# New per-half tiles, new engine lists and a moved addition in a four-layer attention and expert kernel on one core

## The reference, cut to what matters

```python
x0 = x; y = ln_c(x)                            # no gain, no bias
for i in range(4):
    x_s = attention(layernorm(y, gs, bs), w_qkv_s, w_out_s, b_out_s)      # over 64 positions
    x_t = attention(layernorm(y + x_s, gt, bt), w_qkv_t, w_out_t, b_out_t)  # over 16 times
    y = layernorm(x_s + x_t, gf, bf) + y
t = x0 + y
probs = softmax(ln_t(t) @ Wr); w, idx = top_k(probs, 2)
out = t + sum over the two experts of w * (gelu(ln_t(t) @ W1[e]) @ W2[e])
```

## Time and profile before

| | |
|---|---|
| three runs | 665.67, 669.15 and 670.98 us; median 669.15 us |
| profiled execution, own time | 671.71 us |
| its span | 669.9 us |
| mean granted TensorE clock | 0.913 |
| TensorE busy | 550.3 us, 82% |
| VectorE busy | 454.9 us, 68% |
| ScalarE busy | 305.9 us, 46% |
| GpSimd busy | 249.0 us, 37% |

### The profile page before, as it was taken

How to read it: one execution, slowest core, us unless ns; L and a number is a source line. 1 busy time by engine, 2 the same in 40 slices (tenths; PEclk the granted TensorE clock), 3 DMA queues, 4 the chain that set the end, 5 groups by cost and what they waited for, 6 DMA issues and landing times.

```text
span 669.9 us, 21398 instructions
## 1 busy us (share of the span) xinstructions
PE 550.3 (82%) x8984; PEld 432.4 (65%) x8984; DVE 454.9 (68%) x1336; ACT 305.9 (46%) x507; POOL 249.0 (37%) x197
## 2 busy tenths in 40 slices
PE   0978988897898977978988798889888736999991
PEld 0565676566756846665677467746766635999991
DVE  5586847948877576788755966986479676444444
ACT  1455833274466433744844256448434313343330
POOL 6403501441253031613700424154014273777642
PEclk9999979799999897989979979999798575999996
DMA  4000008400000100000001000000000014141314
GB/s 134 1 2 1 3 3 298 174 2 18 1 3 4 32 1 4 2 18 1 2 4 33 2 2 3 17 1 3 3 2 3 6 46 110 50 145 53 107 38 141
DMA packets 17425, 24.71 MB, mean 37 GB/s; under 512 B 2578, under 2 KB 12180, under 8 KB 17268
## 3 DMA queue, kind: packets, MB, share of 16 engines
q1 hardware_dynamic: 14836, 18.17, 8.7%
q0 software_dynamic: 2496, 5.18, 2.3%
HBM read 17.12 MB, written 9.33 MB: 39 GB/s over the span
## 4 chain that ended last, share of the span: by engine, by line
PE 63%; DVE 15%; ACT 11%; issue 5%; POOL 2%; DMA 2%; SPq 0%; DVEq 0%; ACTq 0%
PE turn L678 8%; PE small L832 8%; PE score L748 7%; PE score L795 7%; PE small L933 6%; PE score L921 6%; PE small L727 5%; PE turn L695 4%; PE turn L758 4%; PE turn L760 3%; DVE stats L955 3%; ACT probT L626 3%; PE small L868 3%; ACT prob L620 2%; ACT kE L613 2%
## 5 line engine op out<-in xcount | busy, mean ns | idle before, releaser
L499 POOL TENSOR_TENSOR rstd<-veps,mhalf 128x8 f32<-128x8 f32 x28 | 46.5, 1661 | 246.1 <-DVE veps L995 246.1
L626 ACT ACTIVATE probT<-turn 128x512 f32<-128x512 f32 x96 | 53.3, 597 | 94.9 <-PE turn L678 94.7
L1088 DVE TENSOR_REDUCE top<-score 128x16 f32<-128x1024 f32 (+1 forms) x48 | 58.5, 1219 | 39.2 <-PE score L795 39.2
L795 PE MATMUL score<-kE,qT 32*32 32x64 f32 (+1 forms) x3072 | 58.6, 261 | 12.2 <-issue 12.1
L795 PEld LDWEIGHTS score<-kE,qT 32*32 32x32 f32 (+1 forms) x3072 | 48.8, 123 | 27.1 <-issue 26.0
L678 PE MATMUL turn<-ident,prob 128*128 128x128 f32 x384 | 61.2, 311 | 2.9 <-ACT prob L620 2.9
L1090 DVE TENSOR_TENSOR prob<-score,top 128x1024 f32<-128x1024 f32 x48 | 58.8, 1224 | 1.6
L678 PEld LDWEIGHTS turn<-ident,prob 128*128 128x128 f32 x384 | 49.2, 160 | 6.7 <-ACT prob L620 3.6
L549 POOL DMA_INDIRECT answers<-y_sb,home x46 | 44.7, 971 | 23.9 <-DVE y_sb L1224 16.5
L832 PE MATMUL small<-v_s,probT 128*64 128x34 f32 x1024 | 43.0, 240 | 12.5 <-ACT probT L626 6.8
L620 ACT ACTIVATE prob<-prob 128x1024 f32<-128x1024 f32 x48 | 50.1, 1057 | 6.9 <-DVE prob L1090 6.7
(11 more groups left out here) (126 smaller groups left out, 1058.3 us busy)
## 6 DMA issues: line engine op xcount, KB each, us to landing
w_all<-in_w SPq DMA_DIRECT2D x2, 2048.0 KB, 19.9
dispatched<-in_slots_init SPq DMA_DIRECT2D x2, 1518.0 KB, 10.1
slots<-dispatched SPq DMA_DIRECT2D x6, 396.0 KB, 4.6
pairs<-answers SPq DMA_DIRECT2D x8, 256.0 KB, 3.7
ws<-in_w_s SPq DMA_DIRECT2D x4, 257.0 KB, 2.7
wt<-in_w_t SPq DMA_DIRECT2D x4, 257.0 KB, 2.6
x_in<-in_x SPq DMA_DIRECT2D x2, 512.0 KB, 4.3
vec<-in_vec_in SPq DMA_DIRECT2D x4, 256.0 KB, 4.0
```

The source lines that it names most:

```text
L626: nc.scalar.activation(probT[:, q.nth % 2, 2 * k:2 * k + 2, 2 * h:2 * h + 2, :].rearrange("p k g n -> p k (g n)"), turn[:, u % 2, :].rearr ...
L795: last = nc.tensor.matmul(score[b * n:(b + 1) * n, g, c * 2 * n:(c + 1) * 2 * n], qT[rows, tok:tok + n], kE[rows, :, tok:tok + n], start=q ...
L1088: nc.vector.tensor_reduce(tops, mine, AX_X, ALU.max).then_inc(top_ready, 1)
```

## The change

The five residual tiles and `qT` and `kE` become two tiles each, one for each half. All now lie in the arena, each half's next to one another (`halves`, `x_own` and `own` are lists of the two halves). The expert tiles of half 0 lie over the tiles of half 0's residuals (`slots0`, `xT`, `w1_now`, `hT`) and keys (`y_sb`), `slots1` over the rotary tiles. The three expert blocks 0 to 2 stand ahead of `place.e10` and of ScalarE's `normal.e10` in the lists.

In the last layer GpSimd's `bias.f` adds the input to the bias tile in a second instruction, and `final.f` writes into `x_in` directly, signalling after each four chunks; VectorE's addition is gone.

All lists are new. In `ORDERS` TensorE has eight glows before and after, at other places; in `TAIL` eleven before and five after, one of them before tick 19. VectorE's list in `ORDERS` changes by one exchange.

```diff
 "PE" of ORDERS
-        score.s00 more.s00 glow.s06 head.t10- lead.t10- tail.t10- mix.t10- head.s00 score.s01 more.s01 out.t10- lead.s00 tail.s00 mix.s00 head.s01 lead.s01 tail.s01 mix.s01 glow.s05
-        out.s00 turn.s10 project.s10 turn.t00 fold.s10 values.t00 project.t00 values.s10 score.s10 more.s10 fold.t00
-        score.s11 more.s11 head.s10 lead.s10 tail.s10 mix.s10 score.t00 more.t00 head.s11 lead.s11 tail.s11 mix.s11 glow.s02 out.s10 glow.s07 glow.s01 glow.s03
-        head.t00 lead.t00 tail.t00 mix.t00 turn.t10 project.t10 out.t00 fold.t10 score.t10 more.t10 values.t10 glow.s04 turn.s00+ glow.s00
-        project.s00+ fold.s00+ values.s00+
+        score.s00 glow.s00 head.t10- more.s00 lead.t10- tail.t10- mix.t10- score.s01 head.s00 more.s01 out.t10-
+        head.s01 tail.s00 lead.s00 mix.s00 lead.s01 tail.s01 mix.s01 glow.s01 glow.s02 out.s00 turn.s10
+        project.s10 glow.s03 turn.t00 fold.s10 values.t00 project.t00 score.s10 values.s10 more.s10 fold.t00
+        score.s11 more.s11 head.s10 lead.s10 score.t00 tail.s10 head.s11 mix.s10 more.t00 tail.s11 lead.s11
+        mix.s11 out.s10 head.t00 tail.t00 glow.s05 glow.s04 lead.t00 turn.t10 mix.t00 project.t10 out.t00
+        values.t10 fold.t10 score.t10 glow.s07 glow.s06 more.t10 turn.s00+ project.s00+ fold.s00+ values.s00+
 "ACT" of ORDERS
-        head.t10- tail.t10- soft.s00 head.s00 rest.s00 out.t10- soft.s01 tail.s00 head.s01 rest.s01 tail.s01
-        out.s00 normal.s10 turn.s10 normal.t00 turn.t00 values.t00 part.s10 values.s10 soft.s10 part.t00
-        rest.s10 head.s10 tail.s10 soft.s11 rest.s11 head.s11 soft.t00 tail.s11 out.s10 rest.t00 head.t00 tail.t00
-        normal.t10 turn.t10 out.t00 part.t10 normal.s00+ turn.s00+ values.t10 soft.t10 part.s00+ values.s00+
-        rest.t10
+        head.t10- soft.s00 tail.t10- head.s00 rest.s00 out.t10- soft.s01 head.s01 tail.s00 rest.s01 tail.s01
+        out.s00 normal.s10 turn.s10 normal.t00 turn.t00 part.s10 values.t00 values.s10 soft.s10 part.t00
+        head.s10 rest.s10 soft.s11 tail.s10 rest.s11 head.s11 tail.s11 soft.t00 out.s10 rest.t00 head.t00
+        tail.t00 normal.t10 turn.t10 out.t00 part.t10 normal.s00+ turn.s00+ soft.t10 values.t10 part.s00+
+        values.s00+ rest.t10
 "PE" of TAIL
-        project.t10@0 out.t00@0 fold.t10@0 glow.s03@0 values.t10@0 score.t10@0 more.t10@0 turn.e00@0 logits.e00@0
-        head.t10@0 place.e00@0 glow.s00@0 glow.s04@0 lead.t10@0 tail.t10@0 mix.t10@0 glow.s14@0 out.t10@0 turn.e10@0 logits.e10@0
-        place.e10@0
+        score.s10@0 more.s10@0 fold.t00@0 values.s10@0 score.s11@0 head.s10@0 more.s11@0 lead.s10@0 head.s11@0
+        score.t00@0 tail.s10@0 mix.s10@0 more.t00@0 tail.s11@0 lead.s11@0 mix.s11@0 out.s10@0 glow.s00@0
+        head.t00@0 tail.t00@0 lead.t00@0 mix.t00@0 turn.t10@0 project.t10@0 out.t00@0 fold.t10@0 score.t10@0
+        more.t10@0 turn.e00@0 logits.e00@0 values.t10@0 place.e00@0 head.t10@0 lead.t10@0 tail.t10@0 mix.t10@0
+        glow.s01@0 out.t10@0 turn.e10@0 logits.e10@0 place.e10@3 glow.s03@19
 "DVE" of TAIL
-        out.t00@0 stats.f00@0 final.f00@0 stats.e00@0 soft.t10@0 rest.t10@0 rank.e00@0 normal.e00@0 place.e00@0
-        origin.e00@0 place.e10@0 origin.e10@21 merge.e00@47 merge.e10@47
+        out.t00@0 stats.f00@0 final.f00@0 stats.e00@0 soft.t10@0 rest.t10@0 normal.e00@0 rank.e00@0 place.e00@0
+        origin.e00@1 place.e10@3 origin.e10@24 merge.e00@47 merge.e10@47
 "ACT" of TAIL
-        part.t10@0 values.t10@0 turn.e00@0 soft.t10@0 rank.e00@0 head.t10@0 rest.t10@0 normal.e00@0 tail.t10@0
-        out.t10@0 turn.e10@0 rank.e10@0 normal.e10@0
+        part.t10@0 turn.e00@0 soft.t10@0 rest.t10@0 rank.e00@0 normal.e00@0 values.t10@0 head.t10@0 tail.t10@0
+        out.t10@0 turn.e10@0 rank.e10@0 normal.e10@3
 "POOL" of TAIL
-        stats.t10@0 project.t10@0 stats.f00@0 stats.e00@0 bias.f10@0 send.e00@0 send.e01@0 send.e02@0 send.e03@0
-        send.e04@0 stats.f10@0 send.e05@0 send.e06@0 send.e07@0 stats.e10@0 send.e10@0 send.e11@0 send.e12@0
-        send.e13@1 send.e14@3 send.e15@3 send.e16@3 send.e17@3
+        stats.t10@0 project.t10@0 bias.f10@0 stats.f00@0 stats.e00@0 send.e00@0 send.e02@0 send.e01@0 send.e06@0
+        send.e03@0 send.e07@1 stats.f10@1 send.e05@1 send.e04@1 stats.e10@1 send.e10@1 send.e14@2 send.e11@2
+        send.e15@2 send.e17@3 send.e16@4 send.e13@5 send.e12@8
...
+        slots0 = at("slots0", [P, BLOCKS, ROW], 20480)
+        xT = at("xT", [P, 2, XGROUP * P], 20480 + 12160)
+        w1_now = at("w1_now", [P, WAYS, FF], 20480 + 12160 + 4096)
+        hT = at("hT", [P, 2, FF], 20480 + 12160 + 8192)
+        y_sb = at("y_sb", [P, ANSWERS, P], keys)
+        slots1 = at("slots1", [P, BLOCKS, ROW], 0)
...
+                    if last_f:
+
+                        pool.wait_ge(lifted, q.half + 1)
+                        nc.gpsimd.tensor_tensor(x_bias[q.half][:, :, :], x_bias[q.half][:, :, :], x_own[q.half],
+                                                ALU.add).then_inc(bias_ready, 1)
...
-                        nc.vector.tensor_tensor(half_of(x_in, q.half), half_of(x_in, q.half), half_of(x_res, q.half),
-                                                ALU.add).then_inc(add_ready, 1)
-                        dve.wait_ge(add_ready, q.half + 1)
...
+                    closing = q.layer == DEPTH - 1
+                    dst = (x_own if closing else x_res)[q.half]
                     for c in range(HC):
...
+                        if closing and c % 4 == 3:
+                            last.then_inc(add_ready, 1)
```

More of the change, by code:

```diff
@@ L112 @@
         stats.s10 divide.s01 normal.s10 out.s00 stats.t00 normal.t00 project.s10 project.t00 soft.s10 rest.s10
-        soft.s11 rest.s11 divide.s10 soft.t00 rest.t00 divide.s11 out.s10 stats.t10 normal.t10 divide.t00
+        soft.s11 rest.s11 divide.s10 soft.t00 divide.s11 rest.t00 out.s10 stats.t10 normal.t10 divide.t00
         divide.t01 project.t10 out.t00 stats.f00 final.f00 stats.s00+ soft.t10 normal.s00+ rest.t10 project.s00+
@@ L131 @@
     "PE": """
[L132 to L138 removed]
+        score.s00@0 head.t10-@0 more.s00@0 lead.t10-@0 tail.t10-@0 score.s01@0 mix.t10-@0 more.s01@0 out.t10-@0
+        head.s00@0 tail.s00@0 lead.s00@0 mix.s00@0 tail.s01@0 head.s01@0 glow.s04@0 lead.s01@0 mix.s01@0
+        glow.s02@0 out.s00@0 turn.s10@0 project.s10@0 turn.t00@0 fold.s10@0 project.t00@0 values.t00@0
+        score.s10@0 more.s10@0 fold.t00@0 values.s10@0 score.s11@0 head.s10@0 more.s11@0 lead.s10@0 head.s11@0
[3 more added lines that the diff above has]
+        glow.s01@0 out.t10@0 turn.e10@0 logits.e10@0 place.e10@3 glow.s03@19
     """,
@@ L141 @@
         soft.s00@0 rest.s00@0 divide.t10-@0 divide.t11-@0 soft.s01@0 rest.s01@0 out.t10-@0 stats.f10-@0
-        divide.s00@0 final.f10-@0 stats.s10@0 divide.s01@0 normal.s10@0 out.s00@0 stats.t00@0 normal.t00@0
+        divide.s00@0 final.f10-@0 divide.s01@0 stats.s10@0 normal.s10@0 out.s00@0 stats.t00@0 normal.t00@0
         project.s10@0 project.t00@0 soft.s10@0 rest.s10@0 soft.s11@0 rest.s11@0 divide.s10@0 soft.t00@0
-        rest.t00@0 divide.s11@0 out.s10@0 stats.t10@0 normal.t10@0 divide.t00@0 divide.t01@0 project.t10@0
@@ L148 @@
     """,
     "ACT": """
-        head.t10-@0 soft.s00@0 tail.t10-@0 rest.s00@0 out.t10-@0 head.s00@0 tail.s00@0 soft.s01@0 rest.s01@0
-        head.s01@0 tail.s01@0 out.s00@0 normal.s10@0 turn.s10@0 normal.t00@0 turn.t00@0 part.s10@0 values.t00@0
-        values.s10@0 part.t00@0 soft.s10@0 rest.s10@0 head.s10@0 tail.s10@0 soft.s11@0 rest.s11@0 head.s11@0
-        soft.t00@0 tail.s11@0 rest.t00@0 out.s10@0 head.t00@0 tail.t00@0 normal.t10@0 turn.t10@0 out.t00@0
-        part.t10@0 values.t10@0 turn.e00@0 soft.t10@0 rank.e00@0 head.t10@0 rest.t10@0 normal.e00@0 tail.t10@0
@@ L155 @@
-        out.t10@0 turn.e10@0 rank.e10@0 normal.e10@0
+        head.t10-@0 tail.t10-@0 out.t10-@0 soft.s00@0 rest.s00@0 head.s00@0 tail.s00@0 soft.s01@0 rest.s01@0
+        tail.s01@0 head.s01@0 out.s00@0 normal.s10@0 turn.s10@0 normal.t00@0 turn.t00@0 part.s10@0 values.t00@0
+        part.t00@0 soft.s10@0 values.s10@0 head.s10@0 rest.s10@0 soft.s11@0 head.s11@0 tail.s10@0 rest.s11@0
+        tail.s11@0 soft.t00@0 out.s10@0 rest.t00@0 head.t00@0 tail.t00@0 normal.t10@0 turn.t10@0 out.t00@0
+        part.t10@0 turn.e00@0 soft.t10@0 rest.t10@0 rank.e00@0 normal.e00@0 values.t10@0 head.t10@0 tail.t10@0
@@ L156 @@
+        out.t10@0 turn.e10@0 rank.e10@0 normal.e10@3
     """,
     "POOL": """
[L158 to L161 removed]
+        bias.s00@0 stats.f10-@0 stats.s10@0 stats.t00@0 project.s10@0 project.t00@0 bias.s10@0 bias.f00@0
```

121 lines of the change are left out of this document (54 added, 67 removed).

## The result

The changed kernel took 662.84 us in the median of four runs (656.77 to 668.85), the kernel before, measured beside it, 669.59 (665.67 to 670.98): a ratio of 0.986, 95% interval 0.982 to 0.990. That lies in the predicted range, at its slow end. Twelve later runs gave 669.85 (659.48 to 674.43) against 669.76 for the kernel before, a ratio of 0.995 (0.991 to 0.999); their median lies outside the range. In all ratios here runs more than 1.5% above the fastest of their kernel are left out; medians are of all runs. So the gain is between nothing and 1.4%, where 18.3 us, 2.7%, were forecast. Of the two profiles the one after is 8.0 us shorter in span.

A forecast was written before the change was run, and what follows sets the result against it. No engine alone was the bound: four fixed lists hand work on, a waiting entry holding up its engine. Layers' 15.3 plus last list's 3.0 gave 18.3 us, from 671.7 to 653.4, or 651 from the median 669.15; range 638 to 664.

The forecast's parts named there:

- the layers' term: Lists of layers 0 to 2: 5.4 us won in each of two layers, 4.5 in layer 0, together 15.3.
- the last layer's 3.0 us: Last layer's list, 3.4 plus 0.5 of the first third minus 0.95 for a glow: about 3.0 us won.
- near 123: Sign named for the changed profile: the period of `final.f00`, one layer, near 123 us instead of 128.3.
- rival C: Clock falls as long as before, only somewhere else: 2.6 us a layer and 3 at the end, 658; chance 0.20.
- The hole: TensorE's 1.62 us wait for nothing visible between back-to-back temporal scores; gone at `score.t00`, and 1.6 more at `more.t10`.
- the 4.5: Layer 0's gain in us, below 5.4, as no half layer before it fills the wait of `head.s01`.
- rival D: TensorE idles 3 us at `head.s01` before `lead.s00`, then half clock; six in each of four layers, about 675; chance 0.10.
- The step on `values.t10` ahead of the fold: End of each layer's list: `values.t10` before `fold.t10` loses about 2.5 us there, wins 3.5 before the next layer's `turn`.
- until `out.t00` about 3.4: Last layer's first two thirds: about 3.4 us earlier, gains smaller since `head.s11` still waits behind ScalarE's `values.s10`.
- The moved addition, net 1.3 lost: Last layer, half 0: `final.f00` waits 2.5 us for GpSimd's power, against 1.22 removed from VectorE: loss 1.3.
- Early blocks, 3.4 won: Expert blocks 0 to 2 ahead of `place.e10`: half of 6.7 us goes, block 4 starts 3.4 us earlier.
- as long as now: Sign of being wrong: TensorE's half-clock stretches in the changed profile are as long as in the kernel before.

The follow-up runs named there:

- the second profile: The changed kernel run again with no edit, twelve runs: median 669.85 us, ratio 0.995 to the kernel before.
- the pair of profiles above: Changed kernel's first profile against a kernel with last layer's middle resequenced, half 1's GpSimd additions later and layers' temporal scores back to back, 663.11 us.
- the fastest kernel: Changed kernel with last layer's middle in the layers' sequence, half 1's GpSimd additions later and layers' `values.t10` back behind `more.t10`: 654.19 us, 0.976 to the kernel before.

## Why the prediction held, and where it failed

The first four runs lie in the range, at its slow end, 11.8 us above the forecast; the twelve later ones lie outside it. So that it held is in part luck. Of the 18.3 us that were added up, the layers' term was too large by far, and of the last layer's 3.0 us nothing is seen.

- **Layers, 15.3 forecast.** The period of 121.7 and 122.6 us is the "near 123" that was named, but the last layer's projection starts 11.7 earlier, not 15.3; in the second profile the two periods are 122.7 and 124.5, and on average of seven profiles the three layers win 4.6. What is won goes with the falls of the clock. Of the gains of the order itself, for which even rival C counted 2.6 a layer, nothing is left at a like half-clock time. The `lead` at 1.15 us is as forecast. The hole did not go: it moved into `score.t10` (376.11, 1.43 us of "issue") and into `values.t10` (367.04, 1.17). It was counted twice as a gain, 1.6 each, as if it belonged to the scores standing back to back; it belongs to a place in TensorE's instruction stream (last section). In layer 0 the 4.5 were 3.0: `head.s01` waits 2.28 us for the exponential, the place of rival D, which otherwise didn't come.
- **The step on `values.t10` ahead of the fold** was mis-sized: 2.5 lost and 3.5 won were forecast, a net gain. From the output projection to the fold the three layers lose 2.6, 3.7 and 4.0, and with the step taken back the three layers are some 6 us shorter, by one profile. That is about what the order wins elsewhere, 5.2 us with the temporal scores by the pair of profiles above. The wait for the banks (0.30) was seen; the hole between small matmuls (1.17) was counted as a gain elsewhere and not as a cost here. Without this step, and with the last layer's middle and additions mended, the kernel takes 654.19. That this is near the 651 forecast for the change confirms nothing: it is another kernel.
- **Last layer, "until `out.t00` about 3.4".** This failed: that list runs the heads of s11 ahead of the temporal scores, and behind the wait for ScalarE in front of them, which the prediction mentions as the reason for smaller gains, the clock fell for 24 us. VectorE's sum of `out.t00` came 2.8 us later after the `final.f00` before it, not 3.4 earlier; with the layers' sequence there it came 3.6 earlier, in one profile. A fall was priced at 2.5 us; this one costs 5 to 7.
- **The moved addition, net 1.3 lost.** Right in size and in its way. From VectorE's sum of `out.t00` to `final.f00` it is 8.57 us where it was 6.10: 2.5 longer, as forecast, for GpSimd's power stands behind the two additions and ends at 504.19, and `final.f00` starts at 504.29. The centring, held up by 2.1 us, ends at 504.26, so the lock costs under 0.1 us more, not 0.5; without it `final.f00` would still have waited for the power. At the ranking nothing of the 1.3 is seen: it waits for TensorE's router product. GpSimd's timeline:

```profile
497.70 2.34 POOL L539 TENSOR_TENSOR x_bias<-x_res,vec 128x1024 f32<-128x1024 f32 x1
500.12 2.41 POOL L545 TENSOR_TENSOR x_bias<-x_bias,x_in 128x1024 f32<-128x1024 f32 x1
502.50 1.69 POOL L508 TENSOR_TENSOR rstd<-veps,mhalf 128x8 f32<-128x8 f32 x1
```

  The second of them and the centring are the pair of which the Trainium skill (SBUF — State Buffer, "SBUF: two separate sides") says that they lock each other out. The trace agrees, with VectorE as the one that waits: 2.09 us longer beside GpSimd, back to 2.18 with the additions moved. GpSimd's power, of 128 x 8, does no such thing: with the additions moved it ran from 498.86 to 500.54 beside that centring.
- **Early blocks, 3.4 won.** Block 0 comes earlier and there is a hole of 2.94 us before block 4, both as forecast; but "half of the 6.7 goes" should have been all. Counted from the ranking, block 4 stands at 50.5 us, where it was 50.8 before: `place.e10` also waits on VectorE behind the early blocks' results. The glow before block 19 costs 0.9, as forecast.

Of the rivals, C (the clock falls as long as before, only somewhere else, 658) is the nearest: half-clock time in all is 112 and 125 us in two profiles after, and 119 before, and what left the layers came back in the last layer. The prediction's own sign of being wrong, half-clock stretches "as long as now", was the right test, and it came.

## What to carry to other kernels

In a list written out by hand, look for the idle microsecond ahead of a dense stretch: with it filled, by the order or by idle multiplications, a stretch at half clock that had cost 5 to 7 us did not come, in the few profiles taken. A stage moved off one engine is not free where the other engine's instruction runs beside a two-input one of the first, or where the next step waits behind it; whether it costs time depends on which engine the stage after waits for, here TensorE. Compare two orders at a like half-clock time, or the clock's luck is taken for the order's gain. And before counting a gain of a microsecond in the list, run the unchanged kernel a dozen times: these spread by 15 us, with the clock.

## What the runs showed that was not expected

TensorE stayed at 1.2 GHz for 24 us while it was busy for 23.02 of 25 us: being busy did not bring the clock back there. The falls come at other places and for other lengths in two executions of one kernel: in layer 2's end 6.8 us in one profile of the changed kernel and 13.7 in the next. Holes that wait for nothing visible come inside runs of small matmuls wherever these stand: in `values.t10`, in `score.t10`, and between temporal scores. They keep to a place in TensorE's instruction stream. Counted over its weight loads, multiplications and semaphore instructions in the order of the trace, 131 of the 132 holes of over 0.4 us inside score and projection runs, in the fourteen profiles of this case, lie 193 or 194 instructions behind a multiple of 256. So an order decides only on which work such a place falls. What happens there no run settles, nor whether the fastest kernel gains more without early blocks; that was not tried.
